# Attention on one core: score and maximum products in column tiles of 32, and one tile's sum moved from GpSimd to TensorE

## The reference

```python
x = x + _L0_attn_ref(_layernorm(x, axis=-1), ...)

q = (x @ Wq.T).reshape(b, t, N_HEADS, HEAD_DIM)        # 8 heads of 32
kv_latent = x @ Wkv_down.T                             # rank 64
k = (kv_latent @ Wk_up.T).reshape(b, t, N_HEADS, HEAD_DIM)
v = (kv_latent @ Wv_up.T).reshape(b, t, N_HEADS, HEAD_DIM)
scores = jnp.einsum('bqhd,bkhd->bhqk', q, k) * HEAD_DIM ** (-0.5)
attn = jax.nn.softmax(scores, axis=-1)
out = jnp.einsum('bhqk,bkhd->bqhd', attn, v)
```

## Time and profile before

| | us |
|---|---|
| median of 3 executions | 2265.46 |
| lowest, highest | 2260.86, 2268.83 |
| profiled execution: span from first to last instruction | 2203.9 |
| profiled execution: what lies around its span | not recorded; the median is 61.6 above the span |
| TensorE busy, of the span | 1734.9 (79%) |
| GpSimd busy | 1509.8 (69%) |
| VectorE busy | 1469.4 (67%) |
| ScalarE busy | 1187.6 (54%) |

### The profile page before, as it was taken

One profiled execution on the slowest core, in us unless ns is written; L12 is line 12 of the kernel. 1 busy time (PEld: TensorE's weight loads), 2 busy tenths in 40 slices (PEclk: granted clock), 3 DMA queues, 4 the chain that ended last, 5 costly groups with the idle time before them and its releaser, 6 DMA issues. The chain is left out here.

```text
span 2203.9 us, 47779 instructions
## 1 busy us (share of the span) xinstructions
PE 1734.9 (79%) x12049; PEld 979.0 (44%) x12049; DVE 1469.4 (67%) x3940; ACT 1187.6 (54%) x2321; POOL 1509.8 (69%) x1151
## 2 busy tenths in 40 slices
PE   7979999999999999996772799377777766100997
PEld 3423433444444444333662688244444444000897
DVE  5756878888788887882787244178888887620453
ACT  4626777777777777775562355234444444021343
POOL 0006999999999999995677333588888883155565
PEclk9978999999999999998555899699999998555999
DMA  5753221222212222221242233400000000132232
GB/s 157 248 173 109 62 62 58 60 60 61 64 58 60 61 60 65 58 69 55 95 142 83 94 126 126 141 20 20 19 19 19 19 19 1 43 113 98 84 105 60
DMA packets 158016, 167.97 MB, mean 76 GB/s; under 512 B 39521, under 2 KB 124392, under 8 KB 157960
## 3 DMA queue, kind: packets, MB, share of 16 engines
q1 hardware_dynamic: 143128, 137.02, 20.3%
q0 software_dynamic: 13824, 29.43, 4.2%
q10 hardware_dynamic: 1008, 0.92, 0.1%
HBM read 93.57 MB, written 73.97 MB: 76 GB/s over the span
## 5 line engine op out<-in xcount | busy, mean ns | idle before, releaser
L764 DVE TENSOR_REDUCE halfmax<-p_m 128x1 f32<-128x512 f32 x1024 | 640.4, 681 | 169.7 <-PE p_m L637 169.6
L751 ACT ACTIVATE probs<-p_s,ESCALE 128x512 f32<-128x512 f32 x1024 | 621.7, 691 | 103.1 <-PE p_s L661 100.1
L591 POOL TENSOR_TENSOR sum_p<-sum_p,probs 128x1024 f32<-128x1024 f32 x256 | 604.8, 2362 | 17.2 <-ACT probs L751 1.1
L637 PE MATMUL p_m<-ka,qa 96*128 96x512 f16 x1024 | 398.5, 391 | 14.2 <-DMA vh<-v 12.0
L661 PE MATMUL p_s<-qa,ka 98*128 98x512 f16 x1024 | 392.2, 386 | 10.3 <-ACT probs L751 4.4
L666 PE MATMUL p_o<-probs,vh 128*32 128x256 f32 x4096 | 275.6, 387 | 0.0
L1647 PE MATMUL ln_p_cum<-ln_kv,c_tri 128*128 128x512 f32 (+1 forms) x384 | 163.8, 570 | 91.6 <-POOL ln_kv L1591 91.6
L1304 ACT ACTIVATE e_h<-e_p_h,e_w 128x256 f32<-128x256 f32 x316 | 126.3, 474 | 172.8 <-PE e_p_h L1283 172.5
L661 PEld LDWEIGHTS p_s<-qa,ka 98*128 98x128 f16 x1024 | 99.5, 98 | 214.2 <-ACT probs L751 125.8
L591 POOL TENSOR_TENSOR sum_p<-probs 128x1024 f32<-128x1024 f32 x64 | 150.8, 2356 | 60.6 <-ACT probs L751 60.6
L1220 POOL DMA_INDIRECT xs<-r_xn,r_slot x128 | 125.7, 982 | 69.3 <-issue 35.1
(11 more groups left out here) (299 smaller groups left out, 2718.3 us busy)
## 6 DMA issues: line engine op xcount, KB each, us to landing
e_xb<-xs SPq DMA_DIRECT2D x40, 257.0 KB, 2.7
e_xb<-xs SPq DMA_DIRECT2D x78, 128.0 KB, 2.0
ys<-e_y SPq DMA_DIRECT2D x78, 128.0 KB, 1.9
v<-pj_v SPq DMA_DIRECT2D x8, 1024.0 KB, 4.9
qa<-q SPq DMA_DIRECT2D x64, 128.0 KB, 2.6
ka<-k SPq DMA_DIRECT2D x64, 128.0 KB, 2.7
vh<-v SPq DMA_DIRECT2D x64, 128.0 KB, 2.1
o<-ot SPq DMA_DIRECT2D x64, 128.0 KB
```

The costliest lines, as they stand in the source:

```text
L591: nc.gpsimd.tensor_tensor(sum_p[s % 2][:, :], (sum_p[s % 2] if n else probs[0])[:, :], probs[k][:, :], ALU.add).then_inc(sum_p_d, 1)
L637: nc.tensor.matmul(max_bank(s, n)[:, :], qa[s][0:KA, (n // 2) * P:(n // 2 + 1) * P], ka[s][0:KA, (n % 2) * HALF:(n % 2 + 1) * HALF], start ...
L751: nc.scalar.activation(probs[k][:, h * HALF:(h + 1) * HALF], score_bank(s, k, h)[:, :], ACT.Exp, scale=ESCALE[:, 0:1]).then_inc(probs_d, 1)
L764: nc.vector.reduce_max(halfmax[s % 2][:, n // 2, n % 2:n % 2 + 1], max_bank(s, n)[:, :], AX.X).then_inc(max_read, 1)
```

## The change

The maximum and the score products are each split into four products of 32 columns of weights, at the column tiles 0, 32, 64 and 96, with the same moving operand for all four. They write the four groups of 32 partitions of the same bank. The first of the four stands behind the wait, the last raises the semaphore. The turn of the row maxima, a transpose before, becomes a product with the identity at the column tile 0. `POOL_SUMS` loses its last entry, so that GpSimd adds four times (key tiles 0 to 4), and `denominators` takes key tiles 5, 6 and 7. The steps still hold two key tiles.

```diff
--- before.py
+++ after.py
@@ -406,7 +406,7 @@
     return next(d for d in range(1, len(banks)) if banks[i - d] == banks[i])
 
 
-POOL_SUMS = (1, 2, 3, 4, 5)
+POOL_SUMS = (1, 2, 3, 4)
 
 
 def attend(nc, c, q2, k2, v0, o0, inv0, W0, w, ESCALE, wo, wg, oT):
@@ -634,8 +634,12 @@
             if n == 0:
                 pe.wait_ge(operands_in[s], (r + 1) * LOADS * 16)
             max_bank_read(pe, u, max_place(s, n))
-            nc.tensor.matmul(max_bank(s, n)[:, :], qa[s][0:KA, (n // 2) * P:(n // 2 + 1) * P],
-                             ka[s][0:KA, (n % 2) * HALF:(n % 2 + 1) * HALF], start=True, stop=True).then_inc(max_scores, 1)
+            for j in range(4):
+                mm = nc.tensor.matmul(max_bank(s, n)[j * DH0:(j + 1) * DH0, :],
+                                      qa[s][0:KA, (n // 2) * P + j * DH0:(n // 2) * P + (j + 1) * DH0],
+                                      ka[s][0:KA, (n % 2) * HALF:(n % 2 + 1) * HALF], start=True, stop=True,
+                                      tile_position=(0, j * DH0))
+            mm.then_inc(max_scores, 1)
 
         def max_turn(pe, r, s):
 
@@ -643,7 +647,8 @@
             pe.wait_ge(max_row, u + 1)
             if exists(r, s, 1):
                 max_bank_read(pe, u + 1, turn_place(s))
-            nc.tensor.transpose(turn_bank(s)[0:KT, 0:P], rowmax[:, :], c["ident"][:, :]).then_inc(max_T, 1)
+            nc.tensor.matmul(turn_bank(s)[0:KT, 0:P], rowmax[:, :], c["ident"][:, :], start=True, stop=True,
+                             tile_position=(0, 0)).then_inc(max_T, 1)
 
         def score_bank(s, k, h):
 
@@ -657,8 +662,12 @@
             read = u * SCORES + 2 * k + h - last_use(SCORE_BANKS, s * SCORES + 2 * k + h) + 1
             if not (isinstance(read, int) and read <= 0):
                 pe.wait_ge(probs_d, read)
-            cols, q = slice(k * P, (k + 1) * P), slice(h * HALF, (h + 1) * HALF)
-            nc.tensor.matmul(score_bank(s, k, h)[:, :], ka[s][:, cols], qa[s][:, q], start=True, stop=True).then_inc(scores, 1)
+            q = slice(h * HALF, (h + 1) * HALF)
+            for j in range(4):
+                cols = slice(k * P + j * DH0, k * P + (j + 1) * DH0)
+                mm = nc.tensor.matmul(score_bank(s, k, h)[j * DH0:(j + 1) * DH0, :], ka[s][:, cols], qa[s][:, q],
+                                      start=True, stop=True, tile_position=(0, j * DH0))
+            mm.then_inc(scores, 1)
 
         def spread(pe, s, col, lhs, rhs, start, stop):
 
```

## The result

The changed kernel took 2300.3 us (median of 4, 2291.54 to 2309.87), the kernel before 2264.02 beside it: **1.016 times** as long, with a 95% interval of 1.013 to 1.019. The forecast was 2231 us and a gain; its range ended at 2262.

A forecast was written before the change was run, and what follows sets the result against it. TensorE, edge to edge, was taken to set 13.06 us per head; the terms gave 12.53, so -0.53 x 64 heads = -34 us, span 2203.9 to 2170, plus 61.6: 2231 us, range 2212 to 2262.

The forecast's parts named there:

- What bounds the kernel: Attention stage: TensorE's products stand edge to edge and set the 13.06 us per head; GpSimd is nearly full but waits.
- (1): Maximum and score products: each becomes a group of four 32-column products, taking 0.217 us like the full-width product.
- The branch's 0.3 us per four heads stays.: TensorE's loop over the heads: 0.3 us per four heads, put down to the loop's branch, remains after the change.
- (2): Edges around `p_o`, where column tiles change width: they vanish, -0.25 us per ordinary step, -1.00 per head at most.
- (3): Turn of the row maxima: as a product 0.11 us longer, hidden by VectorE's chain; the step takes 2.98, not 3.22.
- (4): Long step: GpSimd's fifth sum goes, -2.36 us off the path; TensorE's extra denominator tile adds 0.43 on the path.
- GpSimd's five sums as the next bound: Attention heads: had the fifth sum stayed, GpSimd's 12.4 us of work per head would meet the new period.
- (5): VectorE's and ScalarE's work in a 2.60 us step: bank releases still come in time; only a 0.03 us slip.
- The distance between span and median: Whole kernel: the runs' median, 2265.46, lies 61.6 us above the profiled span, and this distance was kept.
- the rival of the dearer group: Each head's 32 product groups: exposed waits and loads make a group cost over 0.217; 2334 us, or 2283; chance 0.10.
- The estimate by the Trainium skill's 62 ns per product: Product groups: at about 62 ns per product a group takes 248 ns, 1.0 us per head, 30 us slower overall.

The follow-up runs named there:

- experiment 2: The kernel before the change with only TensorE's loop over the heads written out: 1.000 (0.998 to 1.002) of the kernel before; attention ends at 1021.5.
- experiment 1: The changed kernel with only TensorE's loop over the heads written out: 0.985 of the kernel before, 0.987 on another chip; attention ends at 987.8.

## Why the prediction was wrong

- **What bounds the kernel.** Right: TensorE, edge to edge.
- **(1) A group of four costs 0.217.** Right as array time. This is nevertheless the step that failed: "the order on TensorE stays, with x4 where x1 stood" was costed by what the array does with the groups, and not by what the x4 does to the instruction stream. The pass grew from 1089 to 1929 instructions, past the size, between 1541 and 1749, up to which TensorE kept it. From there on the branch back waits for instructions. 14 times 4.7 us, +66 us, have no term in the sum. Of the one shown 3.1 us are waiting for instructions and some 1.4 are the products at half clock behind it.
- **"The branch's 0.3 us per four heads stays."** Wrong in cause: it is there without a branch (experiment 2), and the branch itself cost nothing measurable as long as the pass stayed resident, that is, was not fetched again. By the trace it is one score product of the fourth head, whose bank is used again after two score products and not three. The size was right: it stayed, 0.32.
- **(2) The edges go.** Right: 0.25 per step. The tile size is their cause and not the type, since f16 and f32 products still follow each other at `p_o`, now 0.22 apart.
- **(3) The turn is hidden.** Right: 3.01 for 2.98, and no gain from a transpose. One number in it is off: seven groups and the longer turn are 7 x 0.217 + 0.22 = 1.74 and not 1.85. The chain, at 1.89, decides either way.
- **(4) The denominators' 0.43.** Right, alone (+26.5 us for 27) and in the sum. GpSimd's five sums as the next bound: right (12.7 per head).
- **(5) Thinner covers.** They held, but for the score product just named, which waited before as well. The sum of (1) to (5), -34 us, is what experiment 1 measured: 987.8 - 1022.3 = -34.5 in the attention stage, and -32.0 on the other chip. That it agrees to 0.5 us is in part luck. Heads in mid-stage became 0.50 shorter, from 13.14 to 12.64, and not 0.53, which makes 28 us over the 56 heads in the middle. Of the other 6.6 us 2.9 are the last head, which no longer waits for the fifth sum, and this had no term.
- **The distance between span and median.** Wrong: the 61.6 us were no time around the span. In every run on record that lists its span the time is only some 2 us above it, so the profiled execution took about 2206 us by this estimate. Its routing stage takes 134.6 us, as on the chips where the kernel before runs in 2204, and not 193, as where it runs in 2275. The ratio was not harmed, since the median served as base.
- **The rivals.** None named the loop. The rival of the dearer group also had a loss, and named fetching in passing, but put it at 32 places per head. The trace has it at one place per pass, and a group costs 0.217. The estimate by the Trainium skill's 62 ns per product, 30 us slower, came near the result for a reason that isn't there: the pairs of load and product start 54 ns apart in experiment 1 (0.217 for four), and TensorE's groups have no gap.

The balance is -34.5 + 65.7 = +31.2 in the attention stage, while the medians differ by 36.3. The 31.2 lie within the interval of the ratio, 29 to 44 us, and the 5 us between were not followed.

## What to carry to other kernels

When an edit multiplies instructions inside a loop, count the instructions of a pass and look at the profile's instruction queue: none of its packets inside the loop means that the loop is resident, and that room can be used up. Here TensorE's limit lay between 1541 and 1749 instructions. Written out straight, the tiled code was fetched with nearly twice the packets of the code before (85 for 44 in 600 us) and cost nothing. And look at the time of several passes and not of one head: a mean over four was needed to see both the 0.3 us and the 4.7. Last, when a short regular delay appears, look for a bank that comes round too soon before the branch is blamed.

## What the runs showed of the hardware beyond that

- Column tiles: 32 groups of four f16 products with different weights and the same moving data run at 0.217 us per group, 512 columns at full speed; the change of tile width costs 0.09 to 0.13 us at each side (128 to 64 wide in f32: 0.09), and a transpose of 8 columns between 32-wide tiles costs 0.10 at each side.
- Straight code with 54 ns per pair of load and product is supplied without a gap: TensorE is busy 598.3 of 600 us while 85 packets of 16 KB come in.
- After a wait of 3 us the granted clock is at the 1.2 GHz level for part of the next 4.5 us, 0.62 on average. After some the lower level lasts longer, 0.50 over 6.8 us from 511.4 on.
- The routing stage after attention stretches over 134 us on some chips and 193 on another, for identical code.
